# The last layer's two local blocks in one phase: a pipeline over tiles of tokens instead of fourteen phases

## The chip, the cores and the metric

One core of one Trainium2 chip runs the kernel. The metric is the device time of one execution in microseconds (us), the median of several runs. The engines that matter here are TensorE (PE; its weight loads are PEld), VectorE (DVE), ScalarE (ACT), GpSimd (POOL) and SyncE (SP).

## What is computed

The input is four sequences (rows) of 1024 tokens with 128 channels, in f32. A row goes through four layers, each an attention part times the SiLU of a feed-forward part. The change is in the feed-forward part of the last layer, which is itself a small network of two equal blocks (DEPTH = 2, HEADS = 8, DIM_HEAD = 64, WINDOW = 64, HID = 341):

```python
def _layer(x, wqkv, qs, ksc, wo, lg, lb, w1, b1, w2, b2):
    h = shift_token(x)                      # the upper 64 channels come from the token before
    q, k, v = jnp.split(h @ wqkv, 3, axis=-1)   # 8 heads of 64
    q = l2norm(q) * qs
    k = l2norm(k) * ksc
    q, k = rotary_xpos(q, k)
    o = local_attention(q, k, v)            # a token sees itself and the 64 before it
    x = x + o @ wo
    h = shift_token(x)
    h = (h - h.mean(-1, keepdims=True)) / jnp.sqrt(h.var(-1, keepdims=True) + 1e-05) * lg + lb
    a, g = jnp.split(h @ w1 + b1, 2, axis=-1)
    return x + (a * jax.nn.gelu(g, approximate=False)) @ w2 + b2
```

## The kernel before

A hardware loop runs over the four rows. Within a row the work is a sequence of phases; a phase has its own semaphores and buffers, and each engine runs its own list of instructions in it, in the order written, and waits at semaphores. The next phase begins when all engines are through. SP does nothing in the phases of interest but clear the semaphores of the phase before.

`local_block(net, d)` is called for d = 0 and 1. A tile is 128 tokens, so NT = 8 tiles per row. Each call has seven phases, and each goes over all 8 tiles before the next begins:

1. shift (`shift_tokens`, L1896 and L1898): two small matmuls per tile move the upper channels down by one token.
2. l_qkv: the input is turned, and per tile three matmuls give q, k (L1991, bank pair `pq`) and v (L1993). ACT squares q and k (L2024), DVE sums the squares (L2045), ACT takes the root (L2031), DVE the reciprocal (L2052), and DVE multiplies q and k by it (L2059, `aq` and `ak`). The rotation is four operations for each of q (DVE) and k (POOL): L1953, L1957 twice, L1959. PE turns the results (L2010) and ACT copies them out (L1946).
3. l_att: a unit is one tile and four of the eight heads, two units per tile. The scores of a unit are two matmuls for the mask (L2107) and four for the heads (L2112), in `ps`, which has two buffers: the scores of unit u+2 are issued between the transposes of unit u's weights (L2124) and their products with the values (L2137, weights stationary). DVE takes the maximum (L2173), ACT four exponentials (L2163), DVE copies the turned weights (L2185) and divides the output by the sum (L2090).
4. l_wo: the output is turned (L2205), copied (L2226), multiplied by `wo` (L2216) and added to x (L2232).
5. and 6. shift again, and a layer norm (L275 to L306).
7. l_ffn: the two matmuls of the gated hidden layer (L2255, L2256), Gelu (L2272), product (L2282), output matmul (L2261), addition (L2287).

After both calls `gate_update` closes the layer: its first instruction is an ACT table load at L911. `weave`, already in use in other layers, merges several lists of work of one engine by the planned time that each piece yields; the result is a fixed order.

## Time and profile before

| what | value |
|---|---|
| median of 3 runs | 5469.78 us (5459.25 to 5474.28) |
| profiled execution, its own time | 5459.79 us |
| its span, first to last instruction | 5458.1 us |
| mean granted TensorE clock | 0.841 of full speed |
| busy: PE, PEld, DVE, ACT, POOL | 78%, 45%, 56%, 41%, 15% of the span |

The span is four equal rows of some 1364 us, so what happens in the two blocks of one row counts four times. The busy shares are means over stages with different limits.

### The profile page before, as it was taken

The numbers are of one execution on the slowest core, as the hardware profiler recorded it, in microseconds if no ns is written. First come the engines' busy times: TensorE is split into PE (matmuls) and PEld (weight loads), VectorE is DVE, ScalarE is ACT, GpSimd is POOL, SyncE is SP. The second block draws the span as 40 slices with busy tenths as digits, with TensorE's granted clock in tenths as the row PEclk, the third lists the DMA queues.
The fourth block names the chain that finished last, engine by engine and source line by source line (L and its number), as shares of the span: only waits on it lengthen the run. The fifth ranks groups of instructions, "written<-read, shape, count | busy, mean of one in ns | idle before, by whom it ended". The sixth has DMA issues, their size and how long they took to land. (4 is left out here: it accounts for less than half of the span.)

```text
span 5458.1 us, 72559 instructions
## 1 busy us (share of the span) xinstructions
PE 4275.9 (78%) x26000; PEld 2480.5 (45%) x26000; DVE 3066.5 (56%) x6315; ACT 2239.1 (41%) x5020; POOL 820.5 (15%) x892
## 2 busy tenths in 40 slices
PE   6786996788678699678867968967886796996777
PEld 4443334466444333445644433344564443334556
DVE  5554764655555476465555547546555554754665
ACT  3354453333335445333333544633333353553333
POOL 1101020311110102032111010203201101020320
PEclk8798896798789889679877979967987897996798
DMA  3101110000210111000021011100002101010000
GB/s 103 43 19 48 30 40 1 1 1 1 66 43 19 47 30 40 1 1 1 1 67 43 19 48 30 40 1 1 1 1 72 37 19 60 18 40 1 1 1 5
DMA packets 87190, 141.32 MB, mean 26 GB/s; under 512 B 17040, under 2 KB 55184, under 8 KB 84496
## 3 DMA queue, kind: packets, MB, share of 16 engines
q1 hardware_dynamic: 86800, 136.38, 9.0%
q8 instruction: 214, 3.51, 0.3%
q14 instruction: 176, 1.44, 0.1%
HBM read 107.88 MB, written 27.26 MB: 25 GB/s over the span
## 5 line engine op out<-in xcount | busy, mean ns | idle before, releaser
L780 DVE TENSOR_REDUCE mhalf<-mx 128x1 f32<-128x512 f32 (+3 forms) x2064 | 1285.1, 653 | 811.3 <-PE mx L730 438.1
L753 ACT ACTIVATE prob<-ps_st 128x512 f32<-128x512 f32 (+3 forms) x2432 | 1131.6, 512 | 1245.1 <-PE ps_st L694 618.6
L727 PE MATMUL mx<-ks,qs 72*128 72x512 bf16 (+3 forms) x2304 | 849.2, 384 | 249.2 <-issue 79.7
L694 PE MATMUL ps_st<-qs,ks 75*128 75x512 bf16 (+3 forms) x2432 | 784.4, 347 | 26.2 <-ACT prob L753 14.2
L677 PE MATMUL ps_o<-prob,vst 128*32 128x512 f32 (+3 forms) x5376 | 561.7, 499 | 21.3 <-ACT prob L753 15.4
L727 PEld LDWEIGHTS mx<-ks,qs 72*128 72x128 bf16 x2304 | 236.3, 103 | 667.4 <-DVE mhalf L780 421.8
L694 PEld LDWEIGHTS ps_st<-qs,ks 75*128 75x128 bf16 x2432 | 233.9, 99 | 479.2 <-ACT prob L753 303.7
L2163 ACT ACTIVATE pr<-ps,nm 128x192 f32<-128x192 f32 (+1 forms) x512 | 204.7, 412 | 262.6 <-DVE nm L2173 262.6
L2137 PE MATMUL po<-lv,ptr 128*128 128x64 f32 x1920 | 246.2, 282 | 5.6 <-DVE ptr L2185 5.6
L2137 PEld LDWEIGHTS po<-lv,ptr 128*128 128x128 f32 x1920 | 228.5, 195 | 37.0 <-DVE ptr L2185 30.9
L306 PE MATMUL turn<-table,nrm 128*128 128x128 f32 x224 | 63.5, 465 | 226.0 <-DVE nrm L285 226.0
L2185 DVE COPY ptr<-pt 128x512 f32<-128x512 f32 (+1 forms) x256 | 157.5, 653 | 141.6 <-PE pt L2124 141.6
L826 POOL COPY vst<-v_tok 128x256 f32<-128x256 f32 x48 | 21.6, 464 | 1376.2 <-PE ps_o L677 1371.4
L439 POOL MEMSET ks<- 32x2048 uint32 x24 | 42.5, 1797 | 1226.7 <-POOLq L261 1226.7
L2010 PE MATMUL pt<-table,qr 128*128 128x128 f32 x256 | 55.0, 352 | 180.3 <-DVE qr L1959 180.3
L677 PEld LDWEIGHTS ps_o<-prob,vst 128*32 128x32 f32 x5376 | 113.1, 109 | 165.8 <-ACT prob L753 69.1
L806 DVE RECIPROCAL rec<-mx 128x16 f32<-128x16 f32 x96 | 24.7, 257 | 289.1 <-PE mx L739 288.9
L1247 PE MATMUL ff<-stream 128*128 128x128 f32 x1024 | 178.5, 310 | 5.9 <-DVE g_tok L1176 5.9
L1374 POOL TENSOR_SCALAR ffn_small<-in_ch,table 80x128 f32<-80x128 f32 x256 | 148.3, 597 | 209.9 <-PE ff L1503 209.9
L1991 PE MATMUL pq<-stream,xn_ch 128*128 128x512 f32 x256 | 153.1, 728 | 32.1 <-DVE ak L2059 26.2
L1247 PEld LDWEIGHTS ff<-stream 128*128 128x128 f32 x1024 | 159.4, 219 | 23.8 <-issue 15.6
L306 PEld LDWEIGHTS turn<-table,nrm 128*128 128x128 f32 x224 | 40.6, 181 | 246.3 <-DVE nrm L285 231.7
(332 smaller groups left out, 7636.6 us busy)
## 6 DMA issues: line engine op xcount, KB each, us to landing
ks<-k_scr SPq DMA_DIRECT2D x144, 192.0 KB
qs<-q_scr SPq DMA_DIRECT2D x288, 96.0 KB
stream<-stream SPq DMA_DIRECT2D x16, 1152.0 KB, 8.7
k_scr<-prob SPq DMA_DIRECT2D x60, 192.0 KB
stream<-stream SPq DMA_DIRECT2D x16, 512.0 KB, 4.5
stream<-stream SPq DMA_DIRECT2D x8, 993.5 KB, 6.8
stream<-stream SPq DMA_DIRECT2D x8, 993.0 KB, 5.9
q_scr<-prob SPq DMA_DIRECT2D x36, 192.0 KB
```

The source lines that it names most:

```text
L306: last = nc.tensor.transpose(turn[:, t // 4, t % 4 * P:(t % 4 + 1) * P], out[:, t, :], net.ident)
L677: last = nc.tensor.matmul(ps_o[32 * h:32 * h + 32, a - hf * HALF:z - hf * HALF], vst[:, g % 2, kt, h, :], prob[:, b % PROBS, h, a - q0:z - ...
L694: last = nc.tensor.matmul(ps_st[:, u % 3, 0:q1 - q0], ks[g % 2][0:KR, h, kt * P:(kt + 1) * P], qs[g % 2][0:KR, hf, h, q0 - hf * HALF:q1 - ...
L727: last = nc.tensor.matmul(bank[:, j * w:(j + 1) * w], qs[g % 2][0:R, hf, h0 + j, (t - 4 * hf) * P:(t - 4 * hf + 1) * P], ks[g % 2][0:R, h0 ...
L753: nc.scalar.activation(prob[:, b % PROBS, h, 0:q1 - q0], ps_st[:, u % 3, 0:q1 - q0], ACT.Exp, scale=scale).then_inc(S["exped"], 1)
L780: nc.vector.tensor_reduce(mhalf[:, hf, h0:h0 + heads, t - 4 * hf, part], bank[:, 0:heads * (k1 - k0)].rearrange("p (n w) -> p n w", n=head ...
L1247: last = nc.tensor.matmul(self.bank[:, i % 2, t * C:(t + 1) * C], self.h[:, i, j, t * P:(t + 1) * P], W(f"l1_w2_{e}", self.HB, j), start=( ...
L1374: last = nc.gpsimd.tensor_scalar(self.sec_t[:, t % 2, e, :], self.bcs[:, t * P:(t + 1) * P], net.K("slot_id")[0:CAP, e:e + 1], None, ALU.i ...
L1991: last = nc.tensor.matmul(pq[:, t % 2, m, :], x, W(f"l3_wqkv{d}")[:, m * IN:(m + 1) * IN], start=True, stop=True)
L2137: last = nc.tensor.matmul(po[:, t % 2, h * D:(h + 1) * D], ptr[:, w % 2, c, s * P:(s + 1) * P], v_l[:, t - 1 + s, h * D:(h + 1) * D], star ...
L2163: nc.scalar.activation(pr[:, u % 2, c, lo:2 * P], ps[:, u % 2, c, lo:2 * P], ACT.Exp, bias=nm[:, u % 2, c:c + 1], accum_out=den[:, t % 2, ...
L2185: nc.vector.tensor_copy(ptr[:, w % 2, :, lo:2 * P], pt[:, w % 2, :, lo:2 * P]).then_inc(S["copied"], 1)
```

## The change

Both calls of `local_block` become one phase, `local_blocks`, with 16 steps: step s is tile s mod 8 of block s div 8. Every engine gets its order from `weave`, with planned times laid out at PERIOD = 12.0 us per step; a step's work is spread over more than 30 us of that plan, so three steps are in flight. The order that results is fixed. PSUM is handed out one bank at a time: a `Bank` makes PE wait for the reader of its last use. Five such banks serve q, k, everything small (`misc`), all transposes of q, k and the feed-forward (`turn`), and the transposes of the weights (`pt_bank`). There is one buffer of scores, `ps`.

The arithmetic changes in some places. The shift is done while copying the turned input (ACT writes the upper channels one column on). q is not multiplied by its norm: the rotation reads q from PSUM, and the reciprocal root goes into the exponential's scale, with a small multiplication on DVE for its bias. The root is a power of -0.5 on POOL. The tables of the rotation are multiplied by the learned scales per step on POOL. The weights are divided by their sum before they are turned (four operations on DVE per unit), and in the product with the values the values are stationary, two heads side by side in one bank, so that the output comes out turned and its transposes go away. The feed-forward part runs in four pieces of four tiles each (`halves`), in the same phase. The results go to `g_tok` and `v_tok`.

The diff, cut to its core; the whole of `local_block` and `shift_tokens` goes away:

```diff
+class Bank:
...
+    def __init__(self, S, mem):
+        self.S, self.mem, self.reader = S, mem, None
...
+    def take(self, pe, reader, value):
+        if self.reader is not None:
+            pe.wait_ge(self.S[self.reader[0]], self.reader[1])
+        self.reader = (reader, value)
+        return self.mem
...
+PERIOD = 12.0
...
+def local_blocks(net, source, middle, result):
...
+        banks = net.psum("banks", [P, 5, HALF])
+        ps = net.psum("ps", [P, 4, 2 * P])
+        po = net.psum("po", [P, HALF])
+        q_bank, k_bank, misc, turn, pt_bank = (Bank(S, banks[:, i, :]) for i in range(5))
+        o_bank = Bank(S, po[:, :])
...
+        def tensor_projection(pe):
+            for s, d, t in steps:
+                base = PERIOD * s
...
+                yield base + 1.4
...
+                bank = q_bank.take(pe, "q", s + 1)
+                nc.tensor.matmul(bank, x, W(f"l3_wqkv{d}")[:, 0:IN], start=True, stop=True).then_inc(S["qmm"], 1)
+                yield base + 2.3
+                bank = k_bank.take(pe, "kunit", s + 1)
+                nc.tensor.matmul(bank, x, W(f"l3_wqkv{d}")[:, IN:2 * IN], start=True, stop=True).then_inc(S["kmm"], 1)
+                yield base + 3.2
+                bank = misc.take(pe, "v", s + 1)
+                nc.tensor.matmul(bank, x, W(f"l3_wqkv{d}")[:, 2 * IN:3 * IN], start=True, stop=True).then_inc(S["vmm"], 1)
...
+        def tensor_turns(pe):
+            for s, d, t in steps:
+                base = PERIOD * s
+                yield base + 8.6
+                pe.wait_ge(S["q"], s + 1)
+                bank = turn.take(pe, "qt", s + 1)
...
+                yield base + 12.2
+                pe.wait_ge(S["k"], s + 1)
+                bank = turn.take(pe, "kt", s + 1)
...
+        def tensor_scores(pe):
+            for s, d, t in steps:
+                for g in range(2):
...
+                    yield PERIOD * s + (13.6, 18.2)[g]
+                    pe.wait_ge(S["qt"], s + 1)
+                    pe.wait_ge(S["kt"], s + 1)
+                    if u >= 1:
+                        pe.wait_ge(S["exped"], u)
...
+        def tensor_values(pe):
+            def turn_shares(s, t, w):
+                u, half = divmod(w, 2)
+                pe.wait_ge(S["share"], u + 1)
+                bank = turned(pt_bank.take(pe, f"copied{half}", w // 2 + 1))
+                for c in range(2):
...
+            def weigh(s, t, w):
+                j = w % 4
+                pe.wait_ge(S[f"copied{w % 2}"], w // 2 + 1)
...
+                for k in range(first, 2):
+                    for c in range(2):
+                        hd = 2 * j + c
+                        last = nc.tensor.matmul(po[D * c:D * c + D, j * P:(j + 1) * P], v_l[:, t - 1 + k, hd * D:(hd + 1) * D],
+                                                ptr[:, w % 2, c, k * P:(k + 1) * P], start=(k == first), stop=(k == 1))
+                last.then_inc(S["o"], 1)
+
+            for s, d, t in steps:
+                base = PERIOD * s
+                for g, (a, b, c, e) in enumerate(((19.1, 20.4, 20.6, 21.8), (23.7, 25.0, 25.2, 26.4))):
+                    w = 4 * s + 2 * g
+                    yield base + a
+                    turn_shares(s, t, w)
+                    yield base + b
+                    turn_shares(s, t, w + 1)
+                    yield base + c
+                    weigh(s, t, w)
+                    yield base + e
+                    weigh(s, t, w + 1)
+        def tensor_output(pe):
...
+                yield base + 29.2
+                pe.wait_ge(S["och"], s + 1)
+                bank = misc.take(pe, "x1", s + 1)
...
+                yield base + 30.6
+                pe.wait_ge(S["x1"], s + 1)
+                bank = misc.take(pe, "sh", s + 1)
...
+        def ffn_base(f):
...
+            return PERIOD * (4 * f + 3) + 41.0
...
+        def tensor_ffn(pe):
+            three = (turn, k_bank, q_bank)
+            for f, d, c in halves:
+                yield ffn_base(f) - 3.4
+                pe.wait_ge(S["nrm"], 4 * (f + 1))
+                bank = turn.take(pe, "in", f + 1)
...
+                    yield ffn_base(f) + 0.9 * j
+                    pe.wait_ge(S["in"], f + 1)
+                    bank = three[j].take(pe, "gelu", 3 * f + j + 1)
+                    nc.tensor.matmul(bank[0:m, :], W(f"l3_w1{d}")[:, HID + c0:HID + c0 + m], x, start=True, stop=True).then_inc(S["gate"], 1)
...
+                    yield ffn_base(f) + 3.2 + 0.9 * j
+                    bank = three[j].take(pe, "hid", 3 * f + j + 1)
...
+                yield ffn_base(f) + 6.8
+                pe.wait_ge(S["hid"], 3 * (f + 1))
+                bank = turn.take(pe, "ffn", f + 1)
...
+        def scalar_projection(act):
+            for s, d, t in steps:
+                base = PERIOD * s
+                yield base + 0.6
...
+                yield base + 2.6
...
+                nc.scalar.activation(sq[:, s % 2, 0, :], q_bank.mem, ACT.Square).then_inc(S["sq"], 1)
+                yield base + 3.5
...
+                yield base + 4.3
...
+        def scalar_turns(act):
+            for s, d, t in steps:
+                base = PERIOD * s
+                yield base + 9.2
...
+        def scalar_weights(act):
+            for s, d, t in steps:
+                base, lo = PERIOD * s, lows(t)
+                for g, (a, b) in enumerate(((16.4, 21.0), (21.6, 25.6))):
+                    u = 2 * s + g
+                    for i in range(4):
+                        yield base + a + 0.4 * i
+                        if i == 0:
+                            act.wait_ge(S["bias"], u + 1)
+                            if u >= 2:
+                                act.wait_ge(S["tp"], 2 * (u - 1))
+                                act.wait_ge(S["rden"], u - 1)
+                        last = nc.scalar.activation(pr[:, u % 2, slot(i), lo:2 * P], ps[:, slot(i), lo:2 * P], ACT.Exp,
+                                                    bias=nm[:, u % 2, 1, slot(i):slot(i) + 1],
+                                                    scale=ss[:, s % 3, 4 * g + i:4 * g + i + 1], accum_out=den[:, u % 2, slot(i):slot(i) + 1])
+                    last.then_inc(S["exped"], 1)
+                    yield base + b
+                    act.wait_ge(S["tp"], 2 * u + 2)
...
+        def scalar_output(act):
+            for s, d, t in steps:
+                base = PERIOD * s
+                yield base + 27.6
...
+        def scalar_ffn(act):
+            three = (turn, k_bank, q_bank)
+            for f, d, c in halves:
+                yield ffn_base(f) - 7.0
+                act.wait_ge(S["mean"], 4 * (f + 1))
+                nc.scalar.activation(mv[:, :, 1], mv[:, :, 1], ACT.Sqrt, bias=eps[:, 0:1]).then_inc(S["std"], 1)
...
+                    yield ffn_base(f) + 2.4 + 0.01 * j
...
+        def vector_projection(dve):
+            for s, d, t in steps:
+                base = PERIOD * s
+                yield base + 4.4
+                dve.wait_ge(S["sq"], 2 * (s + 1))
...
+                nc.vector.tensor_reduce(ss[:, s % 3, :], sq[:, s % 2, :, :].rearrange("p m (h d) -> p (m h) d", h=H), AX.X, ALU.add).then_inc(S["sum"], 1)
...
+                yield base + 5.8
+                dve.wait_ge(S["inv"], s + 1)
...
+                yield base + 6.5
+                dve.wait_ge(S["tab"], s + 1)
...
+                turn_pairs(nc.vector, "qstep", s, 0, heads(q_bank.mem), rq, qr)
+                dve.wait_ge(S["qstep"], 3 * s + 3)
+                nc.vector.tensor_tensor(qr[:, s % 2, :], qr[:, s % 2, :], rq[:, :], ALU.add).then_inc(S["q"], 1)
...
+        def turn_pairs(ops, stepped, s, m, a, r, out):
+            half = D // 2
+            b = lambda tab, lo, n: tab[:, s % 2, m, lo:lo + n].unsqueeze(1).broadcast_to([P, H, n])
+            ops.tensor_tensor(heads(out[:, s % 2, :]), a, b(tc, 0, D), ALU.mult).then_inc(S[stepped], 1)
+            for lo, other in ((0, half), (half, 0)):
+                ops.tensor_tensor(heads(r[:, :])[:, :, lo:lo + half], a[:, :, other:other + half], b(tsn, lo, half), ALU.mult).then_inc(S[stepped], 1)
...
+        def vector_weights(dve):
+            for s, d, t in steps:
+                base, lo = PERIOD * s, lows(t)
+                for g, (a, b, c) in enumerate(((15.2, 18.2, 19.7), (20.0, 23.0, 24.3))):
+                    u = 2 * s + g
+                    yield base + a
+                    dve.wait_ge(S["s"], u + 1)
+                    if u >= 2:
+                        dve.wait_ge(S["exped"], u - 1)
+                    nc.vector.tensor_reduce(nm[:, u % 2, 0, :], ps[:, :, lo:2 * P], AX.X, ALU.max, negate=True).then_inc(S["max"], 1)
+                    yield base + a + 1.0
+                    dve.wait_ge(S["max"], u + 1)
+                    dve.wait_ge(S["inv"], s + 1)
+                    nc.vector.tensor_tensor(nm[:, u % 2, 1, :].rearrange("p (c j) -> p c j", c=2), nm[:, u % 2, 0, :].rearrange("p (c j) -> p c j", c=2),
+                                            ss[:, s % 3, 4 * g:4 * g + 4].rearrange("p (j c) -> p c j", c=2), ALU.mult).then_inc(S["bias"], 1)
+                    yield base + b
+                    dve.wait_ge(S["exped"], u + 1)
+                    if u >= 2:
+                        dve.wait_ge(S["share"], u - 1)
+                    nc.vector.reciprocal(rden[:, u % 2, :], den[:, u % 2, :]).then_inc(S["rden"], 1)
+                    yield base + b + 0.3
+                    dve.wait_ge(S["rden"], u + 1)
+                    for i in range(4):
+                        last = nc.vector.tensor_scalar(pr[:, u % 2, i, lo:2 * P], pr[:, u % 2, i, lo:2 * P], rden[:, u % 2, i:i + 1], None, ALU.mult)
+                    last.then_inc(S["share"], 1)
+                    yield base + c
+                    dve.wait_ge(S["tp"], 2 * u + 1)
...
+        def vector_output(dve):
+            for s, d, t in steps:
+                base = PERIOD * s
+                yield base + 30.2
...
+        def vector_ffn(dve):
+            three = (turn, k_bank, q_bank)
+            for f, d, c in halves:
+                yield ffn_base(f) - 5.5
+                dve.wait_ge(S["std"], f + 1)
+                nc.vector.reciprocal(mv[:, :, 1], mv[:, :, 1]).then_inc(S["rstd"], 1)
...
+                    yield ffn_base(f) - 5.2 + 0.4 * i
...
+                    yield ffn_base(f) + 4.4 + 0.8 * j
+                    dve.wait_ge(S["gelu"], 3 * f + j + 1)
+                    dve.wait_ge(S["mm"], 3 * f + j + 1)
...
+                yield ffn_base(f) + 9.4
+                dve.wait_ge(S["outp"], f + 1)
...
+        def pool_keys(pool):
+            half = D // 2
+            for s, d, t in steps:
+                yield PERIOD * s + 1.0
...
+                yield PERIOD * s + 5.5
+                pool.wait_ge(S["sum"], s + 1)
+                nc.gpsimd.tensor_scalar(ss[:, s % 3, :], ss[:, s % 3, :], 1e-24, None, ALU.max).then_inc(S["floor"], 1)
+                pool.wait_ge(S["floor"], s + 1)
+                nc.gpsimd.tensor_tensor(ss[:, s % 3, :], ss[:, s % 3, :], power[:, :], ALU.pow).then_inc(S["inv"], 1)
+                yield PERIOD * s + 6.6
+                pool.wait_ge(S["kunit"], s + 1)
+                pool.wait_ge(S["tab"], s + 1)
...
+                turn_pairs(nc.gpsimd, "kstep", s, 1, heads(ak[:, s % 2, :]), rk, kr)
...
+                weave(tensor_projection(pe), tensor_turns(pe), tensor_scores(pe), tensor_values(pe), tensor_output(pe), tensor_ffn(pe))
...
-                for d in range(2):
-                    local_block(net, d)
-                gate_update(net, net.xn_tok)
+                local_blocks(net, net.xn_tok, net.g_tok, net.v_tok)
+                gate_update(net, net.v_tok)
             store(net, out[b].rearrange("(t p) c -> p t c", p=P))
```

## Rows read from the trace of the kernel before

**Rows 1.** Busy time by stretch: one shift, l_qkv and l_att; length, busy us by engine, clock
```profile
1003.40:1008.10 4.70, 3.53 (x30) 3.42 (x30) 0.69 (x1) 0.63 (x1) 0.00 (x0) 1.00 0.00 0
1008.10:1074.50 66.40, 40.34 (x120) 21.14 (x120) 55.27 (x72) 24.64 (x50) 41.74 (x38) 0.80 0.00 0
1074.50:1141.10 66.60, 64.01 (x520) 53.81 (x520) 40.75 (x65) 28.33 (x129) 0.00 (x0) 0.94 0.01 1
```

**Rows 2.** Timeline: end of the second block's l_ffn, start of gate_update
```profile
1368.36 0.69 DVE L2287 TENSOR_TENSOR xn_tok<-po,xn_tok 128x512 f32<-128x512 f32 x1 [1.92 <-PE po L2261]
1369.39 1.28 ACT L911 ACT_TABLE_LOAD   x1 [5.71 <-PEq L2243]
```

**Rows 3.** Timeline: DVE and POOL in one tile of l_qkv
```profile
1024.00 0.69 DVE L2059 TENSOR_TENSOR aq<-pq,ss 128x512 f32<-128x512 f32 x1
...
1025.21 1.21 DVE L2045 TENSOR_REDUCE ss<-sq 128x16 f32<-128x1024 f32 x1
...
1025.37 1.27 POOL L1953 TENSOR_TENSOR kr<-ak,tc 128x512 f32<-128x512 f32 x1 [2.32 <-DVE ak L2059]
1026.33 0.85 DVE L1953 TENSOR_TENSOR qr<-aq,tc 128x512 f32<-128x512 f32 x1
...
1026.59 2.03 POOL L1957 TENSOR_TENSOR rk<-ak,tsn 128x256 f32<-128x256 f32 x2
1027.11 1.80 DVE L1957 TENSOR_TENSOR rq<-aq,tsn 128x256 f32<-128x256 f32 x2
...
1028.71 1.33 POOL L1959 TENSOR_TENSOR kr<-kr,rk 128x512 f32<-128x512 f32 x1
1028.95 1.64 DVE L1959 TENSOR_TENSOR qr<-qr,rq 128x512 f32<-128x512 f32 x1
```

**Rows 4.** Timeline: one unit of l_att and the start of the next
```profile
1105.57 1.04 PE L2124 MATMUL pt<-table,pr 128*128 128x128 f32 x8
...
1106.21 1.29 DVE L2185 COPY ptr<-pt 128x512 f32<-128x512 f32 x2 [1.00 <-PE pt L2124]
1106.34 0.21 PEld L2107 LDWEIGHTS ps<-local_qk_bf,ident_bf 128*128 128x128 bf16 x2
...
1106.87 0.63 PEld L2112 LDWEIGHTS ps<-lkt,lqt 64*128 64x128 f32 x8 [0.32 <-issue]
...
1107.72 2.00 PE L2137 MATMUL po<-lv,ptr 128*128 128x64 f32 x16
1107.84 0.96 DVE L2173 TENSOR_REDUCE nm<-ps 128x4 f32<-128x768 f32 x1 [0.34 <-PE ps L2112]
1108.83 0.42 ACT L2163 ACTIVATE pr<-ps,nm 128x192 f32<-128x192 f32 x1 [1.86 <-DVE nm L2173]
...
1109.55 1.04 PE L2124 MATMUL pt<-table,pr 128*128 128x128 f32 x8
...
1110.33 0.21 ACT L2163 ACTIVATION_READ_ACCUMULATOR pr<-ps,nm 128x1 f32 x1
```

**Rows 5.** Timeline of PE: values by column groups, in another layer
```profile
104.71 0.86 PE L677 MATMUL ps_o<-prob,vst 128*32 128x256 f32 x16
```

**Rows 6.** Timeline of PE: 512-column matmuls at full clock; the feed-forward's output
```profile
1014.49 1.88 PE L1991 MATMUL pq<-stream,xn_ch 128*128 128x512 f32 x4
...
1016.21 1.02 PE L1993 MATMUL pv<-stream,xn_ch 128*128 128x512 f32 x2
...
1178.31 5.52 PE L2261 MATMUL po<-stream,h 128*128 128x128 f32 x48
```

**Rows 7.** Groups by line and form, first block of the first row
```profile
L2226 ACT ACTIVATE och<-pt 128x512 f32<-128x512 f32 x8 | 4.7, 596 | 12.3 <-PE pt L2205 12.3
...
L2232 DVE TENSOR_TENSOR xn_tok<-po,xn_tok 128x128 f32<-128x128 f32 x8 | 2.3, 292 | 9.8 <-PE po L2216 9.8
...
L285 DVE TENSOR_SCALAR nrm<-ctx_tok,mv,rstd 128x128 f32<-128x128 f32 x8 | 2.1, 339 | 0.0
```

578 lines of the change are left out of this document (221 added, 357 removed).

## The prediction

> **What bounds the kernel now.** I read the page's busy shares first (PE 78%, DVE 56%, ACT 41%), then cut one row of the input into stretches. The two blocks run from 1003.40 us to the table load at 1369.39 us [rows 1, 2], which is 366.0 us per row and 1464 us of the span. Two phases carry most of a block. In l_qkv (66.4 us for 8 tiles) DVE is busy 55.3 us and POOL 41.7: the norms and the rotation set the pace. In l_att (66.6 us for 16 units) PE is busy 64.0 us at a clock of 0.94, and PE is the limit [rows 1]. The timeline of one unit shows how PE gets there: the next unit's transposes start 3.98 us after this one's (1105.57 to 1109.55), and PE hardly waits, because the scores of a later unit fill the time in which DVE copies, and because maximum and exponentials work on the other score buffer [rows 4]. So the profile before has one engine full in each large phase and another idle. A merger could win much. What decides is whether the new order keeps an engine full.
>
> **The engines' loads in the new phase**, per step (one tile of one block), with durations from the rows. PE: q, k and v at 0.86 us each, since two instructions less take 1.88 − 1.02 [rows 6], 2.6; twice two masks and four scores, 1.37 each (1106.34 to 1107.72), 2.75; 24 transposes at 0.11 (eight per 0.9), 2.7; values, below, 2.0; output, shift and the turned input 1.6; the feed-forward per half of a block some 8.3 (six 0.86, output 2.7 [rows 6], transposes 0.5), a quarter of it 2.1. Sum 13.7 us. DVE: squares' sum 1.2, k's norm 0.7, rotation of q 2.6, two maxima 1.9, two copies 1.3, eight divisions 2.6, the rest (additions, statistics, norm, gated product) some 2.8. Sum 13 us [rows 3, 4, 7]. ACT some 11. If some engine were always busy, a step would cost about 14 us, where now it costs 366/16 = 22.9.
>
> **Values stationary.** Before, 8 products of a unit took 1.8 us (1107.72 to 1109.55) [rows 4]. In another layer 16 instructions of 256 columns with 32-column weights took 0.86 us [rows 5]; one after the other, at 0.43 us per 512 columns, they would take 3.4. So column groups run side by side here, and I take 0.45 us for a unit half, 0.9 per unit, plus small gaps: a mask followed by scores leaves the loader idle 0.32 us [rows 4].
> The Trainium skill, "TensorEngine Tiling (Array Packing)", section Available Configurations, says the same (two independent tiles of 128x64), but its Key Properties say that a change of tiling mode drains the engine, which speaks against this change, as each half of a unit now goes in and out of it. By the drain alone a unit half would stay near 0.8 us and a step would be 0.7 us longer than below.
>
> **The chain through one step.** This is the part on which I rest. I put the planned times of all lists in order (12.0 us apart, ties to the first list) and followed who waits for whom. With one score buffer, one bank for the turned weights and fixed orders, the two units of a step go through the engines almost one after the other. From the end of unit 0's scores of a tile to the same point one step later, at full clock:
> 1. PE: k, a product with values, v, and its arrival: 0.86 + 0.5 + 0.86 + 0.15 = 2.4. ACT's order puts the square of k, the output copy and v's copy (planned 3.5, 3.6, 4.3) ahead of the exponentials (4.4), though their bias is ready after 1.3.
> 2. ACT copies v, 0.6 [rows 7], then four exponentials, 1.75 (1108.83 to the last accumulator at 1110.54) [rows 4]: 4.75.
> 3. DVE: reciprocal 0.2, x's addition 0.29 [rows 7], then q's rotation ahead of the division (both are planned at 6.5 and the projection's list comes first). All its inputs in SBUF and POOL at work, the rotation took 0.85 + 1.80 + 1.64 = 4.3 [rows 3]. Three of the four now read q from PSUM, as the multiplication by the norm did in 0.69 [rows 3]; I take 0.69 + 0.8 + 1.1 = 2.6, between 2.1 (the addition also 0.6) and 4.3. Then four divisions of 192 columns at 0.3: 128 columns take 0.34, start to start 0.27 [rows 7]; with overhead 1.3, between 1.1 and 1.5. Now 9.15.
> 4. Four transposes to the start of the copy 0.64, with the hop 0.8; DVE copy 0.65; the other four transposes (one bank, so they wait for the copy) 0.8; ACT copies them and q, 1.2: 12.6. DVE's maximum and the bias fit inside.
> 5. Exponentials of unit 1, 1.75; reciprocal and division 1.5; transposes 0.8; copy 0.65: 17.3.
> 6. PE: transposes 0.6, product 0.5, the next tile's q 0.86 (planned 1.4, ahead of the scores at 1.6), scores 1.37: 20.7 us.
> Engine loads of 13 to 14 us lie inside 20.7, so none of them bounds the step. The floor and the power on POOL have no row of before. Each costs between 0.2 (the accumulator read, the smallest operation) and 1.0 (POOL's 256 columns) [rows 3, 4]; the pair lies between the sums and k's norm and has some 0.5 us of slack beside the exponentials, so it adds 0 to 1.3; I take 0, since 16 columns are nearer the small row. PE has 7.3 us in this chain and idles some 3 us twice in the step. In l_qkv, with PE busy 61% and waits of that size, the mean clock was 0.80 [rows 1]. That adds 0 to 1.8; I take 0.6. **P = 21.3 us.** The tables' products (six small ones on POOL per step) lie beside DVE's wait.
>
> **The feed-forward inside the pipeline** falls into steps 4f+5 and 4f+6. The root comes between the second and third exponential: two table loads of 1.28 [rows 2] and itself, 2.8. Reciprocal and two norms ahead of the copy 1.0. The transposes of q need the `turn` bank, whose reader is the first gated product, and DVE has that behind unit 1's bias; with the reload for the exponentials, 3.6. Another product ahead of the division, 0.75. The output matmul, 2.7 [rows 6], and its addition ahead of k's transposes in the same bank, 3.8. Sum 12; some overlaps, I take F = 11, between 7 and 13. Three pieces lie in the stream, the fourth in the tail.
>
> **Sum.** Filling the pipeline up to the first maximum 17 us (k's path: transpose, matmuls, sums, rotation of 4.6 on POOL [rows 3], transposes, scores). From the last tile's maximum to the end 37 (two units without projections 17, output, shift and statistics 4, norm 4, feed-forward 12). Fifteen steps between them, two of them narrower by 1.5: 17 + 15 × 21.3 − 3 + 3 × 11 + 37 = 403.5 us per row, against 366.0 now. The thirteen boundaries of phases that go away, and the shifts of 4.7 us [rows 1], are in the 366 already. 37.5 × 4 = 150 us more: 5459.8 + 150 = **5610 us**. The profiled execution lies 10 us under the median of 5469.8, within the spread of the runs, and I leave it so. Break-even is P = 18.8.
>
> **Rivals.**
> - *The pipeline bounds by an engine* (other side). If the waits overlap more than I read, DVE and PE set the step. At the bare load of 14 us, with F = 6: 17 + 210 − 3 + 18 + 37 = 279 per row, 5459.8 − 348 = 5112 us. More likely is a step of 17 (each unit hides part of the other): 339 per row, 5352 us. For it: no engine is over 70% loaded in my chain. Against it: every wait in the chain is between neighbours in a written order. It decides below P = 18.8. Chance of faster 0.22.
> - *The chain holds and its unknown parts are at their lower ends*: P = 19.8, F = 7: 369 per row, 5472 us, no change. Chance of within 0.3%, 0.06.
> - *Contention and the clock decide*: rotation at 4.3 (POOL slows DVE as before) and the clock at 0.80 for the whole chain: P = 24.2, F = 11: 447 per row, 5784 us. Against it: three of four operations take one input from PSUM. Chance 0.1, inside slower.
> - *Column groups do not overlap*: two products in the chain cost 0.4 more each, P = 22.1, 5658 us. Chance 0.08, inside slower.
> Slower in all 0.72. The chain's own range is P from 19.8 to 22.9: 5470 to 5710. To leave out no more than two in ten I reach into the rival: 5310 to 5720. Differences under 0.3% (16 us) can't be told from none here.
>
> **What would show it.** In the profile after: 16 equal steps; the distance between first exponentials of a tile (21 us if right, 14 if an engine bounds); PE under 70% busy in the phase with two waits per step for DVE's divisions; DVE waiting for ACT's exponentials and for PE; the rotation of q between reciprocal and divisions; the phase 400 us long. I am wrong if maxima of the two units lie closer than 9 us, or if the stretch of the blocks is under 360 us per row.

## The result and the profile after

The changed kernel took **5940.4 us** in the median of 3 runs (5932.9 to 5946.1), against 5469.8 before: ratio 1.086, 95% interval 1.083 to 1.090. That is 470.6 us more. The forecast was 5610 with a range to 5720: the sign was right, the size was not.

The page of the profiled execution after (busy time, TensorE's granted clock in tenths by fortieths of the span, then groups: busy us, mean ns of one, and the idle time before them with what ended most of it):

```profile
span 5944.4 us, 72795 instructions
PE 4396.2 (74%) x25504; PEld 2441.1 (41%) x25504; DVE 3001.4 (50%) x6731; ACT 2427.8 (41%) x5284; POOL 1083.3 (18%) x1392
...
PEclk8897985777789798577778979857777897985777
...
L2020 PE MATMUL banks<-table,pr 128*128 128x128 f32 x960 | 237.0, 390 | 427.0 <-DVE pr L2242 375.7
...
L2242 DVE TENSOR_SCALAR pr<-pr,rden 128x192 f32<-128x192 f32 (+1 forms) x512 | 217.5, 486 | 1.8
...
L2314 POOL TENSOR_TENSOR ss<-ss,power 128x16 f32<-128x16 f32 x64 | 187.4, 2928 | 5.3
```

The clock has four stretches of 7, one for each row of the input; the first three slices of each are the new phase. PE's largest idle time is that in front of the transposes of the weights, 427 us, and DVE's divisions end 376 us of it. Further down stand two short operations with long durations: 486 ns for a division of 192 columns, and 2928 ns for the power of 16 columns.

**Where the time came from.** In the first row the blocks run from the first transposes (1011.37 us) to the table load of the next phase (1493.87 us), 482.5 us against 366.0 [rows 1, 2]. That is 116.5 more, times four rows 466: nearly all of the difference. The windows view of that stretch and the 8 us before it (length, busy us by engine, granted clock, DMA share, GB/s):

```profile
core 0: us, PE busy (x) PEld busy (x) DVE busy (x) ACT busy (x) POOL busy (x), PEclk, DMA share, GB/s
1003.40:1493.87 490.47, 319.99 (x1671) 204.28 (x1669) 207.85 (x471) 183.67 (x472) 149.63 (x201) 0.74 0.00 1
```

No engine is near full: PE, at a low clock, 65%, DVE 42%, ACT 37%. Before, PE was busy 64.0 of 66.6 us in l_att and DVE 55.3 of 66.4 in l_qkv [rows 1].

The timeline of one step, from the first maximum of a tile to the first of the next (1108.52 to 1135.60, 27.1 us). First the stretch up to the divisions of unit 0 and the copy of their transposes:

```profile
1108.52 0.96 DVE L2228 TENSOR_REDUCE nm<-ps 128x4 f32<-128x768 f32 x1 [5.13 <-PE ps L2009]
...
1110.20 1.22 DVE L2195 TENSOR_REDUCE ss<-sq 128x16 f32<-128x1024 f32 x1 [0.52 <-ACT sq L2116]
...
1111.70 0.51 ACT L2148 ACTIVATE pr<-ps,nm,ss 128x192 f32<-128x192 f32 x1
1111.84 2.93 POOL L2314 TENSOR_TENSOR ss<-ss,power 128x16 f32<-128x16 f32 x1
...
1113.58 0.21 ACT L2148 ACTIVATION_READ_ACCUMULATOR pr<-ps,nm,ss 128x1 f32 x1
...
1114.80 0.69 DVE L2200 TENSOR_TENSOR ak<-banks,ss 128x512 f32<-128x512 f32 x1 [3.38 <-POOL ss L2314]
1115.41 0.17 DVE L2238 RECIPROCAL rden<-den 128x4 f32<-128x4 f32 x1
...
1115.67 0.68 DVE L2215 TENSOR_TENSOR qr<-banks,tc 128x512 f32<-128x512 f32 x1
...
1116.81 1.84 POOL L2217 TENSOR_TENSOR rk<-ak,tsn 128x256 f32<-128x256 f32 x2
1117.05 1.02 DVE L2210 TENSOR_TENSOR qr<-qr,in_ch 128x512 f32<-128x512 f32 x1
1117.99 2.51 DVE L2242 TENSOR_SCALAR pr<-pr,rden 128x192 f32<-128x192 f32 x4
1118.72 1.38 POOL L2324 TENSOR_TENSOR kr<-kr,rk 128x512 f32<-128x512 f32 x1
...
1120.55 1.12 PE L2020 MATMUL banks<-table,pr 128*128 128x128 f32 x4 [4.02 <-DVE pr L2242]
...
1121.70 0.69 DVE L2249 COPY ptr<-banks 128x512 f32<-128x512 f32 x1 [1.21 <-PE banks L2020]
```

DVE stands 3.4 us on k's norm (L2200) until GpSimd's power is done. The exponentials of unit 0 ended at 1113.79, but their reciprocal is queued behind that norm and starts at 1115.41. Then comes q's rotation, and then four divisions in 2.5 us, beside the keys' rotation on POOL. One by one they take 0.77, 0.31, 1.32 and 0.35 us; the longest runs beside POOL's operation of 1.38. PE waits 4.0 us for them.

The end of the same step:

```profile
1127.34 1.01 DVE L2242 TENSOR_SCALAR pr<-pr,rden 128x192 f32<-128x192 f32 x4
...
1128.40 1.11 PE L2020 MATMUL banks<-table,pr 128*128 128x128 f32 x4 [2.02 <-DVE pr L2242]
...
1132.46 1.92 PE L1970 MATMUL banks<-stream,xn_ch 128*128 128x512 f32 x2
...
1134.21 0.49 PE L2005 MATMUL ps<-local_qk_bf,ident_bf 128*128 128x384 bf16 x2
...
1135.60 0.96 DVE L2228 TENSOR_REDUCE nm<-ps 128x4 f32<-128x768 f32 x1 [5.36 <-PE ps L2009]
```

The divisions of unit 1, with nothing on POOL beside them, take 1.0 us. Behind the wait of 2.0 us PE runs at the lower of its two levels (granted clock 0.51 from 1128.4 to 1134.2): transposes 1.11 us, where four take 0.60 to 0.66 at full clock (below), and q's product 1.92 us, where the two instructions took 1.02 at full clock [rows 6].

### The profile page after: what moved, and what is told of

Same layout as the page of the kernel before. It is cut to its first block and busy times, and to the rows that moved or that the text cites. A ratio compares the mean times of both kernels' runs of the same rounds, so it can differ in the third digit from the quotient of the medians.

```text
span 5944.4 us, 72795 instructions
## 1 busy us (share of the span) xinstructions
PE 4396.2 (74%) x25504; PEld 2441.1 (41%) x25504; DVE 3001.4 (50%) x6731; ACT 2427.8 (41%) x5284; POOL 1083.3 (18%) x1392
## 5 line engine op out<-in xcount | busy, mean ns | idle before, releaser
L2020 PE MATMUL banks<-table,pr 128*128 128x128 f32 x960 | 237.0, 390 | 427.0 <-DVE pr L2242 375.7
L2020 PEld LDWEIGHTS banks<-table,pr 128*128 128x128 f32 x960 | 153.8, 196 | 513.1 <-DVE pr L2242 423.0
L2228 DVE TENSOR_REDUCE nm<-ps 128x4 f32<-128x768 f32 (+1 forms) x128 | 117.7, 920 | 311.8 <-PE ps L2009 311.8
L2148 ACT ACTIVATE pr<-ps,nm,ss 128x192 f32<-128x192 f32 (+1 forms) x512 | 251.8, 506 | 0.5
L2157 ACT ACTIVATE ptr<-banks 128x512 f32<-128x512 f32 (+1 forms) x128 | 73.1, 571 | 381.6 <-PE banks L2020 381.6
L2242 DVE TENSOR_SCALAR pr<-pr,rden 128x192 f32<-128x192 f32 (+1 forms) x512 | 217.5, 486 | 1.8
L2033 PE MATMUL po<-ptr,lv 128*64 128x128 f32 x1920 | 210.2, 367 | 0.4
L2314 POOL TENSOR_TENSOR ss<-ss,power 128x16 f32<-128x16 f32 x64 | 187.4, 2928 | 5.3
L306 PE MATMUL turn<-table,nrm 128*128 128x128 f32 x160 | 45.4, 466 | 191.2 <-DVE nrm L285 191.2
L2033 PEld LDWEIGHTS po<-ptr,lv 128*64 128x64 f32 x1920 | 146.6, 185 | 92.5 <-issue 91.0
```

The lines of the kernel that those rows point to most:

```text
L2020: last = nc.tensor.transpose(bank[:, c, k * P:(k + 1) * P], pr[:, u % 2, half + 2 * c, k * P:(k + 1) * P], net.ident)
L2033: last = nc.tensor.matmul(po[D * c:D * c + D, j * P:(j + 1) * P], v_l[:, t - 1 + k, hd * D:(hd + 1) * D], ptr[:, w % 2, c, k * P:(k + 1) * ...
L2148: last = nc.scalar.activation(pr[:, u % 2, slot(i), lo:2 * P], ps[:, slot(i), lo:2 * P], ACT.Exp, bias=nm[:, u % 2, 1, slot(i):slot(i) + 1 ...
L2242: last = nc.vector.tensor_scalar(pr[:, u % 2, i, lo:2 * P], pr[:, u % 2, i, lo:2 * P], rden[:, u % 2, i:i + 1], None, ALU.mult)
L2314: nc.gpsimd.tensor_tensor(ss[:, s % 3, :], ss[:, s % 3, :], power[:, :], ALU.pow).then_inc(S["inv"], 1)
```

## The experiments

Theory A: a tile's time is one chain of waits through the order in which the work is issued, and an operation costs what of it lies on that chain. Theory B: the new phase is limited by its work, that is by the engines' loads, by contention or by the clock, and another order doesn't help. The kernel before took 5473.7, 5467.1 and 5461.4 us on the chips of these runs. Experiment 9 was run four times, the others once each. The "blocks" given are those of the first row, from the first transposes to the next phase's table load (after: 482.5 us). They are the finer measure: the part outside the blocks is the same code in every run and took 3986 to 4015 us in the profiled executions, most in the changed kernel's own. A difference of two totals holds up to 28 us of that; a table behind experiment 10 has both measures.

**1. The power without its root.** POOL's power is a multiplication by 0.5 of the same size, so the root of both norms is left out.

```diff
-                nc.gpsimd.tensor_tensor(ss[:, s % 3, :], ss[:, s % 3, :], power[:, :], ALU.pow).then_inc(S["inv"], 1)
+                nc.gpsimd.tensor_tensor(ss[:, s % 3, :], ss[:, s % 3, :], power[:, :], ALU.mult).then_inc(S["inv"], 1)
...
-                nc.gpsimd.memset(power[:, :], -0.5).then_inc(S["zero"], 1)
+                nc.gpsimd.memset(power[:, :], 0.5).then_inc(S["zero"], 1)
```


> The power on POOL is replaced by a multiplication by 0.5, so the root of the squares' sum is left out; nothing else changes. Theory A (a step is one chain of waits through a fixed order, about 27 us long): in the changed kernel the power takes 2.93 us and k's norm on DVE waits for it until 1.6 us after the four exponentials are done; the k rotation on POOL also starts 2.9 us earlier and gets out of the way of the divisions. 1.6 to 2.6 us less per step, 60 steps between first and last maxima: 95 to 155 us less than 5940, so 5785 to 5845. Rival B (an engine's load bounds a step): POOL is busy 14 of 27 us and is no bound, so no change, 5930 to 5950. Rival C (the clock is the whole excess): no change either.

Measured 5727.3 us, 213 less than the changed kernel, 205 of them in the blocks: 3.2 us a tile, more than theory A's 1.6 to 2.6 and more than the power's own 2.9. The timeline shows part of the reason:

```profile
1117.77 0.22 POOL L2314 TENSOR_TENSOR ss<-ss,power 128x16 f32<-128x16 f32 x1
1118.03 0.69 DVE L2200 TENSOR_TENSOR ak<-banks,ss 128x512 f32<-128x512 f32 x1 [0.67 <-POOL ss L2314]
1118.80 1.26 POOL L2215 TENSOR_TENSOR kr<-ak,tc 128x512 f32<-128x512 f32 x1 [0.80 <-DVE ak L2200]
1119.75 0.18 DVE L2238 RECIPROCAL rden<-den 128x4 f32<-128x4 f32 x1 [1.03 <-ACT pr L2148]
```

Now the reciprocal waits for the exponentials, not for the norm. POOL's rotation also starts sooner in relation to the divisions, so their mean fell from 486 to 410 ns. With shorter waits the clock of the blocks rose from 0.74 to 0.82.

**2. Divisions ahead of q's rotation.**

```diff
-                    yield base + b + 0.3
+                    yield base + b + 0.25
```


> One planned time is changed (b + 0.3 becomes b + 0.25), so that DVE does the four divisions of unit 0 ahead of q's rotation instead of behind it; the work is the same. Theory A (chain in a fixed order): the transposes of the weights, 1.15 us from start to the copy, are then hidden behind the rotation of 2.4 us, and the copy waits only for DVE; 1.0 to 1.5 us less per step, 60 to 90 us less in all: 5850 to 5880. Rival B (load): no change, since no engine does less, 5930 to 5950.

Measured 5861.5, 79 less (70 in the blocks), in the range. The gain is small because the divisions still stand behind k's norm, and so behind the power, and in the traced step they took 2.9 us beside POOL's rotation.

**3. Keys' rotation cut to one of four operations** (three are left out, the sine products and the addition).

```diff
-                turn_pairs(nc.gpsimd, "kstep", s, 1, heads(ak[:, s % 2, :]), rk, kr)
-                pool.wait_ge(S["kstep"], 3 * s + 3)
-                nc.gpsimd.tensor_tensor(kr[:, s % 2, :], kr[:, s % 2, :], rk[:, :], ALU.add).then_inc(S["k"], 1)
+                nc.gpsimd.tensor_tensor(heads(kr[:, s % 2, :]), heads(ak[:, s % 2, :]),
+                                        tc[:, s % 2, 1, 0:D].unsqueeze(1).broadcast_to([P, H, D]), ALU.mult).then_inc(S["k"], 1)
```


> Three of the four operations of k's rotation on POOL are left out (k is only multiplied by its cosine table). Theory A with contention between POOL and DVE: the divisions of unit 0 take 2.51 us for four while POOL rotates k, and those of unit 1, with POOL idle, 1.01; q's last addition 1.02 against 0.69. Without the rotation 1.8 us less per step, 108 us less: 5820 to 5850. If the divisions of unit 0 are slow for another reason (their data just written), no change. Rival B (load): no change.

Measured 5767.8, 173 less (166 in the blocks) and so more than either theory gave. The group of the divisions in this kernel:

```profile
L2242 DVE TENSOR_SCALAR pr<-pr,rden 128x192 f32<-128x192 f32 (+1 forms) x512 | 129.4, 315 | 1.8
```

486 − 315 = 171 ns over 512 divisions is 88 us. The contention is real and large. The Trainium skill, "SBUF — State Buffer", section Who interferes with whom, has VectorE and GpSimd share one pair of ports under an exclusive lock, so that the loser waits for a whole instruction; for an operation like the division it has this only in a two-port mode, and no run here shows the mode. The single division of 1.32 us beside POOL's operation of 1.38 agrees in kind. Of the other 78 us of the blocks, q's last addition (1.02 before, 0.69 here) makes some 20. The clock rose from 0.74 to 0.79: in the step seen, unit 0's transposes reach their copy in 0.70 in place of 1.15 us. How the rest divides was not taken apart.

**4. TensorE kept awake.** 20 and 10 transposes of the identity, of no use, ahead of the transposes of unit 0 and of unit 1.

```diff
+        def tensor_fill(pe):
+            for s, d, t in steps:
+                for at, n in ((19.05, 20), (23.65, 10)):
+                    yield PERIOD * s + at
+                    bank = turn.take(pe, *(turn.reader or ("kt", s + 1)))
+                    for i in range(n):
+                        nc.tensor.transpose(bank[:, i % 4 * P:(i % 4 + 1) * P], net.ident, net.ident)
```


> PE gets 20 extra transposes of the identity ahead of unit 0's transposes and 10 ahead of unit 1's, into the bank for transposes while it is free, in the two waits for DVE's divisions (4.0 and 2.0 us). They do no work for the result. Rival C (the granted clock is most of what the forecast lacks): PE then comes out of these waits at full speed; transposes to copy 0.75 in place of 1.15 four times, a product with values and q's matmul 1.6 in place of 2.8: about 3 us less per step, 180 us less, 5740 to 5790, with the granted clock of the stretch near 0.95 in place of 0.74. Theory A without the clock: 0 to 60 us more, 5940 to 6000, because some fillers run late.

Measured 5849.6, 91 less (89 in the blocks), between the two ranges. The granted clock of the blocks rose from 0.74 to 0.89, and PE's pieces behind the fill of unit 1 are at full speed:

```profile
1108.88 0.73 PE L2028 MATMUL banks<-table,pr 128*128 128x128 f32 x4
...
1111.63 1.13 PE L1970 MATMUL banks<-stream,xn_ch 128*128 128x512 f32 x2
```

Not all are: the second four transposes of unit 0 still take 1.09 us (1102.91) and the values behind them 1.98, at a granted clock of 0.50. So the low clock follows from the waits and costs at least 1.4 us a tile. It is a part, not the cause: a kernel with PE at 0.89 still stands some 380 us above the kernel before.

**5. No scale in the exponentials** (the queries' norm is left out).

```diff
-                                                    scale=ss[:, s % 3, 4 * g + i:4 * g + i + 1], accum_out=den[:, u % 2, slot(i):slot(i) + 1])
+                                                    accum_out=den[:, u % 2, slot(i):slot(i) + 1])
```


> The exponentials get no scale from memory: q's norm is left out of them. In the changed kernel one takes 0.506 us with it, 0.418 in the kernel before, 0.49 against 0.40 from start to start. Theory A (each term of the chain comes back once per step, and both units' exponentials are in it): 8 × 0.09 = 0.7 us per step, 45 us less than 5940: 5885 to 5905. Rival B (load): ACT is not the bound, no change.

Measured 5848.9, 92 less, but 69 in the blocks. The group of the exponentials, with the scale (changed kernel) and without:

```profile
L2148 ACT ACTIVATE pr<-ps,nm,ss 128x192 f32<-128x192 f32 (+1 forms) x512 | 251.8, 506 | 0.5
```
```profile
L2148 ACT ACTIVATE pr<-ps,nm 128x192 f32<-128x192 f32 (+1 forms) x512 | 204.8, 417 | 0.5
```

A scale read from memory costs 89 ns in each exponential. Eight a tile make 0.71 us and 46 us in all. The Trainium skill, "ScalarE: Activation LUTs", section What ACT_TABLE_LOAD costs, gives about 93 ns for each operand that comes through a pointer; the trace agrees. Here, too, the gain in the blocks is more than the operation's own time, one and a half times it; the clock rose from 0.74 to 0.78. The rest of the 92 lies outside the blocks.

**6. Order alone: q's rotation ahead of k's norm, and the norm behind unit 0's divisions.** Nothing is left out here or in 8.

```diff
                 yield base + 5.8
+                dve.wait_ge(S["tab"], s + 1)
...
+                turn_pairs(nc.vector, "qstep", s, 0, heads(q_bank.mem), rq, qr)
+                dve.wait_ge(S["qstep"], 3 * s + 3)
+                nc.vector.tensor_tensor(qr[:, s % 2, :], qr[:, s % 2, :], rq[:, :], ALU.add).then_inc(S["q"], 1)
+                yield base + 6.6
                 dve.wait_ge(S["inv"], s + 1)
...
-                yield base + 6.5
-                dve.wait_ge(S["tab"], s + 1)
...
-                turn_pairs(nc.vector, "qstep", s, 0, heads(q_bank.mem), rq, qr)
...
```


> The same work in another order on DVE: q's rotation, which does not need the norm, goes to where DVE waits for the power (ahead of k's norm), and k's norm goes behind unit 0's divisions, so that POOL's rotation of k starts after them. Theory A: the divisions start when the exponentials are done, about 1114.3 in place of 1118.0 in the step seen, and take 1.0 in place of 2.5 us: 5.1 us less per step, 300 us less, 5620 to 5680. That is more than the runs without the power or without k's rotation gave one by one, with nothing left out. Rival B (load): no change. Rival C (the power's duration itself must be paid): at most the contention's 1.5 us per step, 5850.

Measured **5581.4**, 359 less (338 in the blocks), and below what any of the three theories gave. Blocks 398.1 us. The divisions' mean is 310 ns and the power is as long as ever:

```profile
1102.30 0.68 DVE L2215 TENSOR_TENSOR qr<-banks,tc 128x512 f32<-128x512 f32 x1
...
1102.80 3.06 POOL L2314 TENSOR_TENSOR ss<-ss,power 128x16 f32<-128x16 f32 x1
...
1104.78 0.18 DVE L2238 RECIPROCAL rden<-den 128x4 f32<-128x4 f32 x1 [0.41 <-ACT pr L2148]
...
1105.05 1.00 DVE L2242 TENSOR_SCALAR pr<-pr,rden 128x192 f32<-128x192 f32 x4
...
1105.96 0.68 DVE L2209 TENSOR_TENSOR ak<-banks,ss 128x512 f32<-128x512 f32 x1
```

Rotation and power both lie beside the exponentials now, the reciprocal waits only 0.4 us, for the exponentials, and the divisions are over before POOL starts on the keys. They take 1.00 us, though most of them lies beside the power. Exchanging two pieces of DVE's list took out the power's wait, the rotation's 2.4 us and the contention.

**7. The same with the fill of experiment 4.**

> The order of e6_rotate_early with the filling transposes of e4_fill. Theory A with the clock as a second, independent term: the 91 us that the fill gave come on top, less where the waits it fills are now shorter (the one ahead of unit 0's transposes falls from 4 to under 1 us, where 20 fillers now run late): between 90 less and 60 more than e6_rotate_early.

Measured 5730.9, 150 more than experiment 6 (133 in the blocks). The clock of the blocks is 0.91, against 0.86, and it doesn't pay: the 20 transposes now start at 1088.46, after the divisions of unit 0 (1086.86 to 1087.86), take 2.35 us, and the real transposes wait behind them until 1090.65. The fill had been free only where PE waited long.

**8. Norm of k behind unit 0's divisions, q's rotation behind unit 1's maximum** (due numbers 6.6 and 9.1 for the two, q's transposes and their copy 11.5 and 11.6, and the gated products that share their bank later).

> Another order: q's rotation goes into DVE's wait for unit 1's exponentials (3.3 us long), q's transposes behind them, k's norm behind unit 0's divisions; the last gate of the feed-forward moves behind it. Theory A: by hand the chain is then 19.5 to 20.5 us with full clock on half of PE's part, 6.5 to 7.5 less than now: 5490 to 5550. Rival B (load): no change.

Measured 5577.1, 4 less than experiment 6 and not the 5490 to 5550 expected. The two orders are not equal, though. The ten steps without feed-forward take 19.2 us in the mean (first maximum to first maximum), near the expected 19.5 to 20.5, where experiment 6 has 20.4. The five with feed-forward in them take 8 us more in all. Moving the last gate put exponentials between the second and the third Gelu, so ACT loads its tables twice more in three of the four pieces, six loads of 1.28 us in a row of the input (groups of this kernel; experiment 6 has 28 and 16 of them):

```profile
L2148 ACT ACT_TABLE_LOAD x40 | 51.3, 1283 | 0.7
...
L2186 ACT ACT_TABLE_LOAD x28 | 35.9, 1283 | 0.3
```

By this count the later rotation gained 1.2 us a step, and the move of the gate that came with it took most of that back.

**9. Another order on all four engines.** Every instruction, wait and buffer is that of the changed kernel. Of the moved numbers, those that carry most:

```diff
-                    yield PERIOD * s + (13.6, 18.2)[g]
+                    yield PERIOD * s + (13.95, 16.5)[g]
...
-                for g, (a, b, c, e) in enumerate(((19.1, 20.4, 20.6, 21.8), (23.7, 25.0, 25.2, 26.4))):
+                for g, (a, b, c, e) in enumerate(((17.3, 23.85, 24.2, -112.2), (25.95, 26.75, -52.25, 27.3))):
...
-                for g, (a, b) in enumerate(((16.4, 21.0), (21.6, 25.6))):
+                for g, (a, b) in enumerate(((18.45, 22.45), (24.6, 29.85))):
...
-                    yield base + a + 0.4 * i
+                    yield base + a + 0.01 * i
```
(A number below that of its stream's last piece means "right behind it".)

> Only the due numbers differ: the same instructions, waits and buffers as the changed kernel, issued in another order on all four engines. It was found by laying the waits of the program out with durations from the traces of this case (exponentials 2.1, power 3.06, rotation on GpSimd 4.3, divisions 1.0 and up to 1.2 more beside that rotation) and moving one number at a time. The same layout gives 421.6 us for a row in the changed kernel's order (490 measured to the start of the gate's stage) and 371 with the rotation ahead of the keys' norm (393 by its time), and 297 here, 315 with TensorE's pieces 15 per cent longer. Theory A (the time is that of one chain of waits through the given order; the engines' own loads are far below it): the measured times stood 1.06 to 1.16 above the layout, so 315 to 345 us a row against 366 in the kernel before, and 5270 to 5390 in all. Theory B (the phase's engine loads, contention and clock make it slower than the separate blocks whatever the order): no better than the 5580 that the best order so far gave, and in no case under 5470.

Measured **5190.7 us** (4 runs, 5181.4 to 5195.3), ratio to the kernel before 0.950, interval 0.948 to 0.952, and 750 us below the changed kernel. Blocks 298.0 us. Windows of nearly that stretch (which begins at 1000.90) and of one step:

```profile
1003.40:1298.93 295.53, 244.32 (x1626) 152.12 (x1624) 184.38 (x468) 174.00 (x465) 138.18 (x190) 0.94 0.00 1
```
```profile
1062.25:1076.85 14.60, 12.88 (x96) 8.04 (x95) 10.28 (x27) 9.03 (x27) 8.39 (x12) 1.00 0.00 1
```

A step takes 14.6 us, PE is busy 12.9 of them, at full clock. The total is 80 us under the lower end of theory A's range. I had allowed for the surplus over the layout that the earlier orders had, and it is gone: 482.5 against 421.6 in the changed kernel, at a clock of 0.74, and 298.0 against 297 here, at 0.94. The timeline of the step:

```profile
1063.64 0.51 ACT L2148 ACTIVATE pr<-ps,nm,ss 128x192 f32<-128x192 f32 x1
...
1064.96 2.93 POOL L2314 TENSOR_TENSOR ss<-ss,power 128x16 f32<-128x16 f32 x1
...
1066.65 1.01 DVE L2242 TENSOR_SCALAR pr<-pr,rden 128x192 f32<-128x192 f32 x4
...
1067.92 0.69 DVE L2209 TENSOR_TENSOR ak<-banks,ss 128x512 f32<-128x512 f32 x1 [0.27 <-POOL ss L2314]
...
1068.12 0.60 PE L2020 MATMUL banks<-table,pr 128*128 128x128 f32 x4
...
1073.94 1.00 DVE L2242 TENSOR_SCALAR pr<-pr,rden 128x192 f32<-128x192 f32 x4
...
1074.70 0.92 PE L2009 MATMUL ps<-lkt,lqt 64*128 64x192 f32 x8
...
1075.55 0.66 PE L2020 MATMUL banks<-table,pr 128*128 128x128 f32 x4
```

The transposes of a unit no longer follow its divisions at once. PE computes the output matmul (unit 0) or the next tile's scores (unit 1) in between, and hardly waits for DVE: the group that had 427.0 us of idle time before it in the changed kernel has 18.9 here.

```profile
L2020 PE MATMUL banks<-table,pr 128*128 128x128 f32 x960 | 157.8, 286 | 18.9 <-DVE pr L2242 10.3 <-DVE ptr L2249 7.8
```

The scores of the next tile stand ahead of the last unit's transposes, so maximum and exponentials run beside the transposes, the copies and the values. That is how the kernel before kept PE full in l_att [rows 4].

**10. The order of 9 with the power as in 1** (the root is left out).

> The order of e9, and GpSimd's power is a multiplication by 0.5, so the root of the norms is left out. In the changed kernel's order this took 213 us away, 3.3 us a tile, the power's whole duration and more. Theory A (a long instruction costs its duration only where the order puts it on the chain): within 60 us of e9, since in e9's order the power lies beside the exponentials and the queries' rotation. Theory B (the power slows what runs beside it, or the load counts): 150 to 210 us under e9.

Measured 5172.0, 19 less (14 in the blocks). The same cut that gave 213 us in the changed kernel's order gives 19 here, one tenth. Theory A.

**The runs side by side.** Blocks and PE's busy time are those of the first row; the gain is that of the blocks of all four rows against the changed kernel.

| run | measured us | blocks us | gain in four rows | PE busy us | clock |
|---|---|---|---|---|---|
| before | 5469.8 | 365.7 | 467 | 287.1 | 0.88 |
| changed | 5940.4 | 482.5 | 0 | 313.1 | 0.745 |
| 1 | 5727.3 | 431.1 | 205 | 292.1 | 0.82 |
| 2 | 5861.5 | 464.9 | 70 | 304.4 | 0.76 |
| 3 | 5767.8 | 440.9 | 166 | 293.1 | 0.79 |
| 4 | 5849.6 | 461.8 | 89 | 333.4 | 0.89 |
| 5 | 5848.9 | 465.3 | 69 | 298.4 | 0.78 |
| 6 | 5581.4 | 398.1 | 338 | 274.1 | 0.86 |
| 7 | 5730.9 | 431.1 | 205 | 322.1 | 0.91 |
| 8 | 5577.1 | 396.7 | 343 | 279.7 | 0.86 |
| 9 | 5190.7 | 298.0 | 738 | 245.4 | 0.94 |
| 10 | 5172.0 | 294.6 | 751 | 244.9 | 0.94 |

PE has the same instructions in all changed kernels but 4 and 7, so its busy time shows how much the clock can have done by itself. From the changed kernel to experiment 9 it fell by 68 of the 184 us of a row, and from 6 to 9 by 29 of 100. The divisions' mean was the same in 6 and 9 (310 and 312 ns), so contention with them had no part in that last step: what is left of its 100 us is waiting that the order took away. In the 184 us it has a part.

## Why the prediction was wrong in size

**Mechanism: right.** Steps 1 to 6 of the chain came in the order that was read out of the due numbers, with the two waits for DVE's divisions and 65% of PE. Experiments 6 and 9 show by order alone that the order sets the time, through the waits and through the contention and the low clock that come with them; 10 shows that the power costs next to nothing where it isn't on the chain.

**The sum.** Blocks 482.5 us against 403.5 forecast. Fill 18.8 (1011.37 to 1030.14; forecast 17). From the last first maximum (1452.87) to the end 41.0 (forecast 37). The fifteen steps between took 422.7 us, forecast 349.5: these 73.2 us are the miss. The ten without feed-forward in them took 26.7 in the mean; with 1.5 given back for each of the two narrow ones that is P = 27.0, where 21.3 was forecast. 15 × 27.0 − 3 = 402.0 leaves 20.7 for the three pieces of feed-forward, 6.9 each and not 11. **So P was too small by 5.7 us (85.5 a row) and F too large by 4.1 (12.3 a row).**

**Two steps of P failed: step 3** ("9.15") **with the power that was added as 0, and the 0.6 for the clock.** By the trace of the step above, counted from the end of unit 0's scores (1108.5):

| up to | forecast | measured | added here |
|---|---|---|---|
| 1, v arrives | 2.4 | 2.7 | 0.3 |
| 2, exponentials of unit 0 | 4.75 | 5.3 | 0.3 |
| 3, divisions of unit 0 | 9.15 | 12.0 | 2.3 |
| 4, copies of transposes and q | 12.6 | 16.6 | 1.15 |
| 5, unit 1 and its copy | 17.3 | 21.7 | 0.4 |
| 6, next scores | 20.7 | 27.0 | 1.9 |

- *Power.* Bounded at 0.2 to 1.0 us by the nearest rows and taken at the small end since it has 16 columns. It took 2.93 us. The upper bound came from POOL's additions and multiplications, none of which says anything of a power, so it wasn't a bound. The slack was larger than the 0.5 us forecast: of some 3.2 us for floor and power, 1.6 came through (reciprocal at 1115.41, exponentials over at 1113.79).
- *Divisions* forecast 1.3 (1.1 to 1.5): 2.5 in unit 0, 1.0 in unit 1. I applied the contention with POOL to the rotation, where the row of before showed it, and not to the divisions, which also read and write SBUF beside the same POOL rotation.
- *Rotation of q* forecast 2.6: 2.4 (1115.67 to 1118.07). The reading that inputs in PSUM spare most of the contention holds, and the rival of 4.3 falls.
- *Exponentials* forecast 1.75 by rows without a scale from memory: 2.1, twice a step (experiment 5).
- *Clock* forecast 0.6 for P, 0 to 1.8: the row of l_qkv gave 0.80; the phase was granted 0.74. Lines 4 to 6 of the table hold the cost, since the transposes and q's product come right after the long waits. An estimate from rows of the step: five groups of four transposes cost some 0.45 us each more than at full clock, a half of the values 0.46, and q's product 0.75, together 3.4 us. By the step seen this is the larger of the two failures. Longer waits lower the clock, and the lower clock lengthens the way to the next wait; I had priced them apart.
- *Values stationary*: forecast 0.45 us a half, 0.5 in the chain. At full clock, in experiment 6:

```profile
1100.42 0.66 PE L2033 MATMUL po<-ptr,lv 128*64 128x128 f32 x8
...
1101.01 1.12 PE L1976 MATMUL banks<-stream,xn_ch 128*128 128x512 f32 x2
```
```profile
1108.59 0.60 PE L1985 MATMUL banks<-table,qr 128*128 128x128 f32 x4
...
1109.12 1.09 PE L2033 MATMUL po<-ptr,lv 128*64 128x128 f32 x16
```

A half by itself takes 0.59 us from its start to the next one's, and both halves in a row (sixteen instructions) some 0.5 each. Four transposes ahead of it last 0.53 to its start, against 0.44 when other transposes follow (experiment 9, 1069.43 to 1069.87). The rival that column groups don't overlap falls, since a half would then take 0.86. The Trainium skill, "TensorEngine Tiling (Array Packing)", section Key Properties, has the engine drain at a change of mode. The trace agrees in kind: a visit costs 0.09 us on the way in and up to 0.16 on the way out (0.59 less the bare 0.43), 0.25 together, not the 0.35 that the prediction put on it from no row. In the chain two halves were so 0.2 us each longer than forecast.
- *Feed-forward* forecast 11 (7 to 13) a piece: 6.9. More of its twelve us overlapped than was read; which part wasn't traced.

**The rivals.** Contention with the clock (5784) was right about the kind of the surplus and wrong about its place, on the rotation. "An engine bounds" was wrong for this order, and right as a statement about the work: with the order of experiment 9 a step takes 14.6 us against the 14 of the bare load, and 5190.7 us lies between its two figures, 5112 and 5352.

**The range** was narrower than its own terms. The upper ends that the prediction names, 1.3 for floor and power (two times 1.0 less 0.5 of slack is even 1.5), 1.8 for the clock and 0.2 for the divisions, on 20.7 make P = 24.0, not 22.9, and 5770 us with F = 11. Contention on the divisions had no room in it at all; with the 1.2 us that it took in place of that 0.2, P = 25.0 and 5830. Even so, 5940 lies beyond.

**What stays open.** The shares of power, contention, scale and clock don't add: experiments 1, 3, 4 and 5 alone gave 213, 173, 91 and 92 us, 569 together (528 in the blocks), more than the whole 470 (467), as each shortens waits that the others need. Over a third of experiment 3's gain wasn't traced. The order of experiment 8 without its extra table loads wasn't run. Whether the separate phases of the kernel before would gain from another order too wasn't tried.

## What to carry to other kernels

When phases are merged into one pipeline with a fixed order, sum the engines' loads, and then walk the chain of the order that is written: the first says what can be had (14 us a step), the second what one gets (27 us). If they lie far apart, reorder before judging the merger: here the same instructions went from 9% slower to 5% faster than the kernel before. Between an operation and the one on another engine that needs it, put a piece that is ready; an operation with an unknown price belongs beside work, not between two engines.

## What the runs showed of the hardware

- GpSimd's power of 128x16 values took 2.93 to 3.07 us, a multiplication of the same size 0.22 us, a maximum with a constant 0.25 us.
- Four DVE divisions of 192 columns in SBUF took 1.0 us alone, 1.0 beside GpSimd's power (experiment 9), and 2.5 to 2.9 us beside GpSimd's rotation. GpSimd's own operation in the rotation went from 1.42 us (experiment 1) to 1.84 us for the pair.
- A half of the values on 64-column weights cost some 0.25 us for going in and out, at full clock.
- Exponentials between two Gelus cost two table loads of 1.28 us (experiment 8).
- A scale read from memory took an exponential of 128x192 from 417 to 506 ns.
- The same instructions in the same phase were granted 0.74, 0.86 and 0.94 of TensorE's clock in three orders. Four transposes at its lower level took 1.1 us, at full clock 0.6 to 0.66. Forcing the clock up with idle work gained 91 us where PE waited 4 us at a time and lost 150 where the idle work reached into the chain.
